# Setup of a one-layer transformer kernel: token rows spread by a matrix product, convolution weights quantised on GpSimd, embedding between parts of the Gram product

## The chip, the core and the metric

The kernel runs on one core of a Trainium2 chip. A core has five engines with an instruction stream each: TensorE (PE, matrix products, with its weight loads shown apart as PEld), VectorE (DVE), ScalarE (ACT), GpSimd (POOL) and SyncE (SP, which here only issues transfers). They share an on-chip memory of 128 partitions (SBUF) and an accumulator memory that TensorE writes (PSUM, 8 banks of 512 fp32 a partition), and meet at semaphores. The metric is the device time of one execution, in microseconds.

## The reference

Integer tokens of shape (2, 1024) go through an embedding with a short convolution, attention and a mixture of experts, each with a residual. Cut to what matters here:

```python
# embedding: both weights are quantised by their largest magnitude / 127
w_emb = fake_quant(emb_weight)                  # (125, 128)
e = w_emb[clip(y, 0)]
x = pad(e, one zero row in front)               # context of 2
w = fake_quant(conv_weight)                     # (128, 1, 2), one pair a channel
h = relu(e_before * w[0] + e * w[1])            # depthwise, per channel
# attention: 8 heads of 64, weights scaled by 1/sigma, one power iteration
v = W @ u / norm; u2 = W.T @ v / norm; sig = v @ W @ u2; Wq = W / sig * sigma
h = h + softmax(mask_diagonal(q k^T * exp(temperature))) v @ Wo.T + b_out
h = h + mixture_of_experts(layernorm(h))
```

`fake_quant(w)` is `w + (round(w / scale) * scale - w)` with `scale = max|w| / 127`.

## The kernel before

The kernel is written per engine, with the order on each engine and every semaphore wait by hand. No planner decides anything.

The layer's body is eight head pairs (four for each of the two sequences). A pair is two heads of eight steps; a step `(k, t)` makes the scores of query tile `t` against all 1024 keys (TensorE, as high and low parts), takes the row maximum (VectorE), exponentials (ScalarE), divides (GpSimd), transposes the probabilities three steps later (TensorE, copied by ScalarE and VectorE), and multiplies them with the values five to six steps later. The projections of the next pair stand between the steps. After the pairs come the experts. None of this is touched but the first step.

The setup in front of it is what the change is about. The stages, with the engine that runs them:

- SP issues the transfers in one queue: embedding table, convolution weights broadcast to 128 partitions, the 1024 tokens of sequence 0 broadcast to 128 partitions, the attention weights by rows (`wr_sb`), the tokens of sequence 1, then all other weights. ScalarE issues the power-iteration vectors `u` and three scalars.
- GpSimd makes constants (`const`, 15 of them: `ones`, `ident`, masks, `vocab_id`, `tie`, `powers`).
- VectorE finds the largest magnitude of each row of the embedding table, and of the convolution weights; `quantise` is four instructions in a chain. The largest over all rows comes from a product on TensorE (`top`). `rows_of(b)` compares each of the 1024 tokens with the partition's number `vocab_id`: a one-hot matrix, vocabulary by position. `table` holds embedding times convolution weight, two taps; both are done at semaphore value `SETUP_TABLES`.
- TensorE: `top`; the Gram product of the 12 row blocks of W, then times `u` (`gu_ps`), which gives W.T W u and so both norms without the transposed pass; `embed(c)` for `c` = 0..3, each eight products (two taps, four tiles of 128 positions) of one-hot columns with `table`; `v_ps`, the output weights times their `u`; the transposes of the normalised first sequence; the projections `dk0`, `dk1`, `dq0`, `dq1` of head 0 (key and query, half 0 and 1); `u2_ps`; and the first scores.
- ScalarE copies each PSUM result: `embedded(c)` with the rectifier, `xt`, the high parts.
- VectorE takes statistics and normalises (`tile_statistics`, `variances`, `normalise_tile`, in groups `NORMS`), GpSimd takes the roots (`deviations`), and VectorE forms the low parts (`first_low`).

`embed(2)` and `embed(3)` are the second sequence, which isn't needed for the first head pair: its statistics are taken in steps (0, 2) to (0, 6) of pair 0.

## Time and profile before

| | us |
|---|---|
| median of 3 runs | 495.35 (495.01 to 495.76) |
| the profiled execution | 495.01 |
| its span, first to last instruction | 493.2 |
| PE / PEld busy | 472.3 (96%) / 404.6 (82%) |
| DVE / ACT / POOL busy | 423.6 (86%) / 363.8 (74%) / 300.6 (61%) |

Over the span the granted TensorE clock is 1.000. The chain that ended last is to 81% TensorE, to 13% VectorE, 2% each waiting for issue, DMA and ScalarE. The busy shares are averages: in the first 12.3 us (a fortieth of the span) TensorE is busy for two tenths of the time, VectorE five, ScalarE one, GpSimd two, and from the second slice on TensorE is at nine tenths or more until near the end. Times in all rows are from the first instruction of the span. A timeline row is: start, length, engine, line, operation, output<-input, count, and in brackets the idle time before it and what ended it. Rows that overlap on TensorE are passes in its pipeline: an fp32 product is two MATMUL records.

### The profile page before, as it was taken

The numbers are of one execution on the slowest core, as the hardware profiler recorded it, in microseconds if no ns is written. First come the engines' busy times: TensorE is split into PE (matmuls) and PEld (weight loads), VectorE is DVE, ScalarE is ACT, GpSimd is POOL, SyncE is SP. The second block draws the span as 40 slices with busy tenths as digits, with TensorE's granted clock in tenths as the row PEclk, the third lists the DMA queues.
The fourth block names the chain that finished last, engine by engine and source line by source line (L and its number), as shares of the span: only waits on it lengthen the run. The fifth ranks groups of instructions, "written<-read, shape, count | busy, mean of one in ns | idle before, by whom it ended". The sixth has DMA issues, their size and how long they took to land.

```text
span 493.2 us, 11360 instructions
## 1 busy us (share of the span) xinstructions
PE 472.3 (96%) x3824; PEld 404.6 (82%) x3824; DVE 423.6 (86%) x722; ACT 363.8 (74%) x688; POOL 300.6 (61%) x357
## 2 busy tenths in 40 slices
PE   2989999999999999999999999999999999999897
PEld 2945788888988898888788898889888988888685
DVE  5469989988998898889998999899989999999465
ACT  1258878887788778877888688878887887683553
POOL 2114697888668866874468857885788556751000
DMA  6500009531953195362622592259225932000002
GB/s 233 218 1 0 2 15 213 127 87 36 200 116 85 34 200 120 85 131 52 126 66 68 108 202 59 73 105 204 56 72 105 202 69 64 0 2 3 3 17 73
DMA packets 29484, 44.78 MB, mean 91 GB/s; under 512 B 3200, under 2 KB 21120, under 8 KB 29184
## 3 DMA queue, kind: packets, MB, share of 16 engines
q1 hardware_dynamic: 28864, 44.21, 38.4%
q8 instruction: 25, 0.41, 0.4%
q14 instruction: 19, 0.16, 0.1%
q10 hardware_dynamic: 576, 0.00, 0.1%
HBM read 6.46 MB, written 1.05 MB: 15 GB/s over the span
## 4 chain that ended last, share of the span: by engine, by line
PE 81%; DVE 13%; issue 2%; DMA 2%; ACT 2%; SPq 0%; POOL 0%; DVEq 0%; ACTq 0%
PE ps L696 22%; PE ps L680 19%; PE ps L662 10%; PE ps L663 10%; PE ps L603 5%; DVE pt_lo L1361 4%; DVE neg_max L1377 4%; PE ps L739 3%; PE ps L598 2%; PE ps L887 2%; DMA arena<-in_wqkv_rows 2%; PE ps L870 2%; PE ps L573 1%; DVE x L1198 1%; PE ps L901 1%
## 5 line engine op out<-in xcount | busy, mean ns | idle before, releaser
L1361 DVE TENSOR_TENSOR pt_lo<-ps,pt_hi 128x512 fp32r<-128x512 f32 x256 | 163.5, 680 | 1.3 <-ACT pt_hi L1036 1.3
L1377 DVE TENSOR_REDUCE neg_max<-ps 128x1 f32<-128x1024 f32 x128 | 156.6, 1223 | 6.5 <-PE ps L667 2.6
L1036 ACT ACTIVATE pt_hi<-ps 128x512 fp32r<-128x512 f32 x256 | 139.3, 596 | 29.4 <-PE ps L680 29.2
L438 POOL TENSOR_SCALAR probs<-probs,inv_sum 128x1024 f32<-128x1024 f32 x128 | 144.6, 1129 | 26.6 <-POOL inv_sum L435 26.6
L696 PE MATMUL ps<-pt_hi,v_slot 128*128 128x256 f32 x512 | 150.0, 324 | 0.0
L1056 ACT ACTIVATE probs<-ps,neg_max 128x1024 f32<-128x1024 f32 x128 | 142.5, 1113 | 6.9 <-DVE neg_max L1377 4.0
L680 PE MATMUL ps<-ident,probs 128*128 128x128 f32 x1024 | 133.7, 273 | 1.5 <-DVE pt_lo L1361 0.9
L680 PEld LDWEIGHTS ps<-ident,probs 128*128 128x128 f32 x1024 | 117.6, 140 | 19.8 <-POOL probs L438 3.0
L696 PE MATMUL ps<-pt_lo,v_slot 128*128 128x256 f32 x512 | 127.8, 282 | 0.0
L435 POOL TENSOR_TENSOR inv_sum<-row_sum,powers 128x1 f32<-128x1 f32 x128 | 70.8, 553 | 83.2 <-ACT probs L1056 83.2
L696 PEld LDWEIGHTS ps<-pt_hi,v_slot 128*128 128x128 f32 x512 | 96.8, 189 | 9.7 <-issue 9.7
L696 PEld LDWEIGHTS ps<-pt_lo,v_slot 128*128 128x128 f32 x512 | 96.7, 189 | 8.8 <-issue 8.8
L662 PE MATMUL ps<-k_hi,q_st 128*128 128x512 f32 x256 | 102.7, 401 | 0.9 <-DVE q_st L1232 0.9
L663 PE MATMUL ps<-k_lo,q_st 128*128 128x512 f32 x256 | 100.8, 394 | 0.0
L1369 DVE TENSOR_TENSOR ps<-ps,neg_block 128x128 f32<-128x128 f32 x112 | 33.4, 298 | 27.3 <-PE ps L663 26.9
L662 PEld LDWEIGHTS ps<-k_hi,q_st 128*128 128x128 f32 x256 | 48.0, 187 | 7.4 <-DVE q_st L1232 1.0
L663 PEld LDWEIGHTS ps<-k_lo,q_st 128*128 128x128 f32 x256 | 48.1, 188 | 6.8 <-issue 1.0
L1049 ACT ACTIVATE arena<-ps 128x256 f32<-128x256 f32 x64 | 24.7, 386 | 36.0 <-PE ps L696 36.0
L428 POOL TENSOR_TENSOR arena<-arena 128x512 fp32r<-128x512 f32 x28 | 35.9, 1282 | 5.2 <-POOL arena L426 5.0
L603 PE MATMUL ps<-xt,w_slot 128*128 128x512 f32 x56 | 28.7, 595 | 0.0
L1056 ACT ACTIVATION_READ_ACCUMULATOR probs<-ps,neg_max 128x1 f32 x128 | 25.3, 198 | 0.0
L395 POOL TENSOR_TENSOR rstd<-rstd,powers 128x4 f32<-128x4 f32 (+1 forms) x6 | 7.5, 1243 | 26.7 <-DVE rstd L1195 26.7
(145 smaller groups left out, 391.6 us busy)
## 6 DMA issues: line engine op xcount, KB each, us to landing
q_st<-arena SPq DMA_DIRECT2D x28, 256.0 KB, 3.8
k_hi<-arena SPq DMA_DIRECT2D x28, 256.0 KB, 5.1
k_lo<-arena SPq DMA_DIRECT2D x28, 256.0 KB, 5.2
v_slot<-v_all SPq DMA_DIRECT2D x14, 512.0 KB, 3.9
arena<-arena SPq DMA_DIRECT2D x28, 256.0 KB, 4.9
f_sb<-in_f SPq DMA_DIRECT2D x2, 1024.0 KB, 10.1
x<-in_tok SPq DMA_DIRECT2D x2, 512.0 KB, 7.6
w_slot<-in_w_pairs SPq DMA_DIRECT2D x8, 128.0 KB, 2.0
```

Source lines behind the costliest of these rows:

```text
L428: pool.tensor_tensor(low.bitcast(F32R), low, high, ALU.subtract).then_inc(qk_split, 1)
L435: pool.tensor_tensor(inv_sum[:, t % 4:t % 4 + 1], row_sum[:, t % 4:t % 4 + 1], powers[:, 3 * NT:3 * NT + 1], ALU.pow).then_inc(recip_done, 1)
L438: pool.tensor_scalar(probs[:, t % 4, :], probs[:, t % 4, :], inv_sum[:, t % 4:t % 4 + 1], 1.0, ALU.mult, ALU.mult).then_inc(norm_done, 1)
L603: return pe.matmul(ps[:, WORK, :], w_slot[:, which, :], xt[:, c * HALF:(c + 1) * HALF], start=True, stop=True)
L662: pe.matmul(bank, q, k_hi[:, k, half], start=True, stop=False)
L663: ins = pe.matmul(bank, q, k_lo[:, k, half], start=False, stop=c != own or not by_pe)
L680: ins = pe.transpose(ps[:, bank, q * P:(q + 1) * P], probs[:, (t - T_LAG) % 4, col:col + P], ident[:, :])
L696: ins = pe.matmul(ps[:, PV_BANK, 0:CW], v_slot[:, slot, jt, :], src[:, c_local % 2, jt, :], start=jt == 0 and src is pt_hi, stop=jt == NT ...
L1036: act.activation(dst, ps[:, transposes_bank(t, a, drain), :].rearrange("p (j c) -> p j c", c=P), ACT.Copy).then_inc(hi_done, 1)
L1056: act.activation(probs[:, t % 4, :].rearrange("p (a c) -> p a c", a=2), ps[:, SCORES + 2 * (t % 2):SCORES + 2 * (t % 2) + 2, :], ACT.Exp, ...
L1361: dve.tensor_tensor(pt_lo[at], ps[:, transposes_bank(t, a, drain), :].rearrange("p (j c) -> p j c", c=P), pt_hi[at].bitcast(F32), ALU.subt ...
L1377: dve.tensor_reduce(neg_max[:, t % 4:t % 4 + 1], ps[:, SCORES + 2 * (t % 2):SCORES + 2 * (t % 2) + 2, :].rearrange("p a c -> p (a c)"), AX ...
```

## The change

1. **Tokens.** The two broadcasts of 512 KB are gone. One transfer puts the tokens as 16 rows of 128 (`tok_sb`, 8 KB). GpSimd clamps them to fp32 and, in `tokens_apart(b)`, writes for each sequence a 16x1024 matrix `tok_diag` that holds row k's tokens in column block k and zero elsewhere (in the memory of `q_st`). `spread_tokens(b)` on TensorE multiplies it by a matrix of ones, which puts all tokens of a sequence on every partition of two PSUM banks, and VectorE makes the one-hot rows from there, in two halves.
2. **Convolution weights.** Their transfer goes first on ScalarE's queue, the tokens second, in front of `u` and the scalars. The scale is still VectorE's; the four instructions of the quantisation are GpSimd's, between `tokens_apart(0)` and `tokens_apart(1)`.
3. **Constants.** GpSimd makes the five that are needed first, and the others after all this; the waits are split accordingly (`N_FIRST_CONST`).
4. **TensorE's order.** Four Gram products, `embed(0)`, tokens of sequence 1, `embed(1)`, the other eight Gram products, `embed(2)`, then `gu_ps`. `embed(3)` is moved behind the first scores. `v_ps` is moved from in front of the transposes to between the projections. The first head's projections are in the order dk0, dq0, dk1, dq1 and in other banks.
5. **ScalarE and VectorE** follow that order; on VectorE `rows_of(1)` is behind the first group's statistics; on ScalarE in the first step the exponentials come before the value copies.

On TensorE, from the first product to the first projection, before (`quant` with `ones` is `top`, `arena` is the Gram product, `table` with `probs` an embedding product, `wo_sb` is `v_ps`, `ident` the transposes):

```order
L568 MATMUL ps<-quant,ones 128x125 [waits setup_dve,const_ready]
L573 MATMUL ps<-arena 128x128 [waits rows_loaded]
L573 MATMUL ps<-arena 128x128 x11
L578 MATMUL ps<-u_sb,arena 128x1 [waits setup_act,u_loaded]
L561 MATMUL ps<-table,probs 128x128 [waits one_hot_ready,setup_dve]
L562 MATMUL ps<-table,probs 128x128
...
L588 MATMUL ps<-u_sb,wo_sb 128x1 [waits wout_loaded]
L588 MATMUL ps<-u_sb,wo_sb 128x1 x3
L593 MATMUL ps<-ident,arena 128x128 [waits xhat_done] x8
L609 MATMUL ps<-xt,arena 128x512 [waits xt_done,h_ready,twice_loaded]
```

and after (`q_st` with `ones_r` spreads tokens):

```order
L617 MATMUL ps<-quant,ones 128x125 [waits setup_dve,const_ready]
L599 MATMUL ps<-q_st,ones_r 128x512 [waits tok_ready]
L605 MATMUL ps<-arena 128x128 [waits rows_loaded]
L605 MATMUL ps<-arena 128x128 x3
L590 MATMUL ps<-table,probs 128x128 [waits one_hot_ready,setup_dve]
...
L599 MATMUL ps<-q_st,ones_r 128x512 [waits tok_ready]
...
L590 MATMUL ps<-table,probs 128x128 [waits one_hot_ready]
...
L605 MATMUL ps<-arena 128x128 x8
L590 MATMUL ps<-table,probs 128x128 [waits one_hot_ready]
...
L632 MATMUL ps<-u_sb,arena 128x1 [waits setup_act,u_loaded]
L612 MATMUL ps<-ident,arena 128x128 [waits xhat_done] x8
L648 MATMUL ps<-xt,arena 128x512 [waits xt_done,h_ready,twice_loaded]
```

The Gram product is cut in two, three of the four embedding groups stand in and behind it, the tokens of a sequence in front of each pair of groups, and `v_ps` is no longer in front of the transposes.

On GpSimd, all that stands between the start and the first root, after:

```order
L381 AFFINE_SELECT ident<-ident 128x128
L390 TENSOR_SCALAR tok_f<-tok_sb 16x128 [waits tok_loaded]
L395 TENSOR_TENSOR q_st<-tok_f,ident 16x1024 [waits tok_ready,const_ready]
L403 TENSOR_SCALAR quant<-conv_sb,qs 125x256 [waits setup_dve]
L405 TENSOR_SCALAR quant<-quant,qs 125x256 [waits conv_steps]
L407 TENSOR_TENSOR quant<-quant,conv_sb 125x256 [waits conv_steps]
L409 TENSOR_TENSOR quant<-conv_sb,quant 125x256 [waits conv_steps]
L395 TENSOR_TENSOR q_st<-tok_f,ident 16x1024
L412 MEMSET ident_b 128x128
...
L424 TENSOR_SCALAR tie<-tie 128x16
L431 TENSOR_TENSOR rstd<-rstd,powers 128x4 [waits aggr_done] x2
```

Before, only the constants stood there (the first root came right behind them). Now the clamp, two spreads of 16x1024 and the four steps on 125x256 do, and the second spread follows the last step with no wait of its own.

On TensorE, the first scores (`k_hi`, `k_lo` with `q_st`) and what follows them, after:

```order
L707 MATMUL ps<-k_hi,q_st 128x512 [waits h_ready,first_lo,const_ready]
L708 MATMUL ps<-k_lo,q_st 128x512
L712 MATMUL ps<-ident_b,neg_diag 128x128
L590 MATMUL ps<-table,probs 128x128
L591 MATMUL ps<-table,probs 128x128
...
L637 MATMUL ps<-wv_sb,xt 128x512 [waits wv_loaded]
L637 MATMUL ps<-wv_sb,xt 128x512 [waits h_ready]
L768 MATMUL ps<-norm_sb,ones 128x2 [waits setup_dve]
```

Before, the rows of `table` weren't there, and the value products (`wv_sb`) followed at once.

The diff, cut to its core:

```diff
+        top, gram_ps, gu_ps = ps[:, 2, 0:VOCAB], ps[:, 3, 0:P], ps[:, 3, 0:1]
+        sums_ps, v_ps, u2_ps, out_sums_ps = ps[:, WORK, 0:2], ps[:, WORK, 4:5], ps[:, WORK, 8:12], ps[:, WORK, 0:2]
...
+        tok_diag = q_st[0:TILES, :, :].rearrange("k b (t n) -> k b t n", n=P)
...
-        EMBED_BANKS = (0, 1, 2, WORK)
-        FIRST_HEAD = {"dk0": WORK, "dk1": TRANS, "dq0": 2, "dq1": TRANS + 1}
+        TOKEN_BANKS = TRANS
+        EMBED_BANKS = (0, 1, 2, TRANS)
+        FIRST_HEAD = {"dk0": 0, "dq0": 1, "dk1": 3, "dq1": TRANS + 1}
...
+            const(pool.memset(ident[:, :], 0.0))
+            pool.wait_ge(const_ready, count[0])
+            const(pool.affine_select(out=ident[:, :], in_=ident[:, :], compare_op=ALU.not_equal, fill=1.0,
+                                     base=0, pattern=[[-1, P]], channel_multiplier=1))
             const(pool.memset(ones[:, :], 1.0))
-            const(pool.memset(ident[:, :], 0.0))
+            const(pool.memset(ones_r[:, :].bitcast(F32), 1.0))
+            const(pool.iota(vocab_id[:, :], [[0, 1]], base=0, channel_multiplier=1,
+                            allow_small_or_imprecise_dtypes=True))
+            assert count[0] == N_FIRST_CONST
+
+            pool.wait_ge(tok_loaded, 16)
+            pool.tensor_scalar(tok_f[:, :], tok_sb[:, :], float(VOCAB - 1), 1.0, ALU.min, ALU.mult).then_inc(tok_ready, 1)
+            pool.wait_ge(const_ready, 2)
+            pool.wait_ge(tok_ready, 1)
+            def tokens_apart(b):
+
+                pool.tensor_tensor(tok_diag[:, b, :, :], tok_f[:, :].unsqueeze(1).broadcast_to([TILES, NT, P]),
+                                   ident[0:TILES, NT * b:NT * (b + 1)].unsqueeze(2).broadcast_to([TILES, NT, P]),
+                                   ALU.mult).then_inc(tok_ready, 1)
+
+            tokens_apart(0)
+            conv_flat = conv_sb[0:VOCAB, :, :].rearrange("p k d -> p (k d)")
+            conv_q = quant[0:VOCAB, D:3 * D]
+            pool.wait_ge(setup_dve, SETUP_CONV)
+            pool.tensor_scalar(conv_q, conv_flat, qs[0:VOCAB, 6:7], ROUND, ALU.mult, ALU.add).then_inc(conv_steps, 1)
+            pool.wait_ge(conv_steps, 1)
+            pool.tensor_scalar(conv_q, conv_q, ROUND, qs[0:VOCAB, 4:5], ALU.subtract, ALU.mult).then_inc(conv_steps, 1)
+            pool.wait_ge(conv_steps, 2)
+            pool.tensor_tensor(conv_q, conv_q, conv_flat, ALU.subtract).then_inc(conv_steps, 1)
+            pool.wait_ge(conv_steps, 3)
+            pool.tensor_tensor(conv_q, conv_flat, conv_q, ALU.add).then_inc(conv_steps, 1)
+
+            tokens_apart(1)
...
-            for m, fill in ((ident, 1.0), (ident_b, 1.0), (neg_diag, NEG), (neg_block, NEG)):
+            for m, fill in ((ident_b, 1.0), (neg_diag, NEG), (neg_block, NEG)):
...
-            sp.dma_start(conv_sb[:, :, :].rearrange("p k d -> p (k d)"),
-                         conv.rearrange("(o k) d -> o (k d)", o=1).partition_broadcast(P)).then_inc(conv_loaded, 16)
-            def tokens(b):
-                sp.dma_start(tok_sb[b], tok[b:b + 1, :].partition_broadcast(P)).then_inc(tok_loaded[b], 16)
-
...
-            tokens(0)
             sp.dma_start(wr_sb, wqkv_rows).then_inc(rows_loaded, 16)
-            tokens(1)
...
+            def spread_tokens(b):
+
+                pe.wait_ge(tok_ready, b + 2)
+                for c in range(2):
+                    pe.matmul(ps[:, TOKEN_BANKS + 2 * b + c, :], ones_r[:, :],
+                              tok_diag[:, b, 4 * c:4 * c + 4, :], start=True, stop=True).then_inc(tok_mm, 1)
...
+            pe.wait_ge(const_ready, N_FIRST_CONST)
             pe.wait_ge(setup_dve, SETUP_DIAG)
             pe.matmul(top, ones[0:VOCAB, :], quant[0:VOCAB, 0:VOCAB], start=True, stop=True).then_inc(setup_pe, 1)
-
-
+            spread_tokens(0)
             pe.wait_ge(rows_loaded, 16)
-            for t in range(12):
-                last = pe.matmul(gram_ps, wr_sb[:, t, :], wr_sb[:, t, :], start=t == 0, stop=t == 11)
-            last.then_inc(setup_pe, 1)
-
+            gram(0, 4)
+            pe.wait_ge(setup_dve, SETUP_TABLES)
+            pe.wait_ge(one_hot_ready, 2)
+            embed(0).then_inc(h_mm, 1)
+            spread_tokens(1)
+            pe.wait_ge(one_hot_ready, 3)
+            embed(1).then_inc(h_mm, 1)
+            gram(4, 12).then_inc(setup_pe, 1)
+            pe.wait_ge(one_hot_ready, 5)
+            embed(2).then_inc(h_mm, 1)
             pe.wait_ge(u_loaded, 16)
             pe.wait_ge(setup_act, 2)
             pe.matmul(gu_ps, gram_sb, u_sb[:, 0:1], start=True, stop=True).then_inc(setup_pe, 1)
-
-            pe.wait_ge(setup_dve, SETUP_TABLES)
-            for c in range(4):
-                if c % 2 == 0:
-                    pe.wait_ge(one_hot_ready, c + 2)
-                embed(c).then_inc(h_mm, 1)
-
-            pe.wait_ge(wout_loaded, 32)
-            for j in range(H // 2):
-                last = pe.matmul(v_ps, wo_sb[:, j, :], u_sb[:, 1 + j:2 + j], start=j == 0, stop=j == H // 2 - 1)
-            last.then_inc(setup_pe, 1)
-
-            for t in range(NT):
-                pe.wait_ge(xhat_done, t + 1)
-                ins = pe.transpose(ps[:, 5 + t // 4, (t % 4) * P:(t % 4 + 1) * P], x_hat[0][:, t, :], ident[:, :])
-                if t % 4 == 3:
-                    ins.then_inc(xt_mm, 1)
+            transpose_rows(0)
+            transpose_rows(1)
...
             pe.wait_ge(twice_loaded, 16)
-            pe.wait_ge(h_ready, 4)
+            pe.wait_ge(h_ready, 2)
             for kind, bank in FIRST_HEAD.items():
-                pe.wait_ge(xt_done, int(kind[2]) + 1)
-                if kind == "dk1":
-                    pe.wait_ge(setup_act, 4)
+                pe.wait_ge(xt_done, 2 if kind == "dq1" else int(kind[2]) + 1)
                 project_twice(kind, 0, bank).then_inc(first_mm, 1)
                 if kind == "dk0":
-
+                    pe.wait_ge(one_hot_ready, 6)
                     pe.wait_ge(setup_dve, SETUP_PRODUCTS)
                     pe.matmul(sums_ps, ones[:, :], norm_sb[:, 18:20], start=True, stop=True).then_inc(setup_pe, 1)
-
-            pe.wait_ge(xt_done, 2)
+                if kind == "dq0":
+                    pe.wait_ge(wout_loaded, 32)
+                    pe.wait_ge(setup_dve, SETUP_RATIO)
+                    for j in range(H // 2):
+                        last = pe.matmul(v_ps, wo_sb[:, j, :], u_sb[:, 1 + j:2 + j], start=j == 0, stop=j == H // 2 - 1)
+                    last.then_inc(setup_pe, 1)
+
+            pe.wait_ge(setup_act, 4)
             for t in range(4):
                 last = pe.matmul(u2_ps[:, t:t + 1], wor_sb[:, t * P:(t + 1) * P], norm_sb[:, 12:13],
                                  start=True, stop=True)
             last.then_inc(setup_pe, 1)
+            pe.wait_ge(const_ready, N_CONST)
 
             def first_values(t):
 
                 for i in (2 * t, 2 * t + 1):
                     if i == 0:
-                        pe.wait_ge(setup_act, 5)
-                    if i == 0:
                         pe.wait_ge(wv_loaded, 16)
+                    if i == 1:
+                        pe.wait_ge(h_ready, 4)
                     if i == 2:
                         pe.wait_ge(first_lo, 4)
...
+                if pair.i == 0 and (k, t) == (0, 0):
+                    embed(3).then_inc(h_mm, 1)
...
+            act.dma_start(conv_sb[:, :, :].rearrange("p k d -> p (k d)"),
+                          conv.rearrange("(o k) d -> o (k d)", o=1).partition_broadcast(P)).then_inc(conv_loaded, 16)
+            act.dma_start(tok_sb[:, :], tok.rearrange("b (t n) -> (b t) n", n=P)).then_inc(tok_loaded, 16)
...
+            embedded(0)
+            embedded(1)
             act.wait_ge(setup_pe, 2)
             act.activation(gram_sb, gram_ps, ACT.Copy).then_inc(setup_act, 1)
+            embedded(2)
             act.wait_ge(setup_pe, 3)
             act.activation(norm_sb[:, 0:1], gu_ps, ACT.Copy).then_inc(setup_act, 1)
-            for c in range(4):
-                embedded(c)
-            act.wait_ge(setup_pe, 4)
-            act.activation(norm_sb[:, 12:13], v_ps, ACT.Copy).then_inc(setup_act, 1)
-            for c in range(2):
-                act.wait_ge(xt_mm, c + 1)
-                act.activation(xt[:, c * HALF:(c + 1) * HALF], ps[:, 5 + c, :], ACT.Copy).then_inc(xt_done, 1)
+            rows_copied(0)
+            rows_copied(1)
...
+                if kind == "dq0":
+                    act.wait_ge(setup_pe, 5)
+                    act.activation(norm_sb[:, 12:13], v_ps, ACT.Copy).then_inc(setup_act, 1)
...
+                            if t == 0:
+                                embedded(3)
+                                exponentials(pair, k, t)
                             first_values(t)
-                            exponentials(pair, k, t)
+                            if t > 0:
+                                exponentials(pair, k, t)
...
-            dve.wait_ge(const_ready, N_CONST)
+            dve.wait_ge(const_ready, 2)
...
-            quantise(conv_flat, quant[0:VOCAB, D:3 * D], 1)
-
-            def rows_of(b):
-
-                dve.wait_ge(tok_loaded[b], 16)
-                dve.wait_ge(const_ready, N_CONST)
-                dve.memset(one_hot[b][:, 0:1], 0.0).then_inc(one_hot_ready, 1)
-                dve.tensor_scalar(one_hot[b][:, 1:SEQ + 1], tok_sb[b], float(VOCAB - 1), vocab_id[:, :],
-                                  ALU.min, ALU.is_equal).then_inc(one_hot_ready, 1)
-
-            rows_of(0)
+            assert count[0] == SETUP_CONV
             dve.wait_ge(setup_pe, 1)
             link(dve.tensor_reduce(qs[0:VOCAB, 1:2], top[0:VOCAB, :], AXX, ALU.max))
             scale(0)
             quantise(emb_sb[0:VOCAB, :], quant[0:VOCAB, 0:D], 0)
+
+            def rows_of(b):
+
+                dve.wait_ge(const_ready, N_FIRST_CONST)
+                dve.memset(one_hot[b][:, 0:1], 0.0).then_inc(one_hot_ready, 1)
+                for c in range(2):
+                    dve.wait_ge(tok_mm, 2 * b + c + 1)
+                    dve.tensor_scalar(one_hot[b][:, 1 + HALF * c:1 + HALF * (c + 1)], ps[:, TOKEN_BANKS + 2 * b + c, :],
+                                      vocab_id[:, :], None, ALU.is_equal).then_inc(one_hot_ready, 1)
+
+            rows_of(0)
...
+                if g == 0:
+                    rows_of(1)
...
-            first_low("dk0")
-            dve.wait_ge(setup_pe, 5)
+            dve.wait_ge(setup_pe, 4)
             ratio(0, sums_ps)
             assert count[0] == SETUP_RATIO
-            first_low("dk1")
+            first_low("dk0")
             dve.wait_ge(setup_pool, 1)
...
-            first_low("dq0")
-            first_low("dq1")
+            for kind in ("dq0", "dk1", "dq1"):
+                first_low(kind)
```

## Rows read from the trace of the kernel before

**Rows 1.** The chain that ended last, to 50 us: start, length, what.
```profile
2.14 7.91 DMA arena<-in_wqkv_rows
...
10.10 4.84 PE ps L573 x24
...
16.06 0.22 PE ps L562 x2
...
22.98 0.79 PE ps L588 x8
...
30.67 0.50 PE ps L662
...
39.52 0.37 ACT v_slot L997
```

**Rows 2.** L573 (ns min/median/max) at 12 and 14 us; busy time with PEclk.
```profile
L573 PE MATMUL ps<-arena x6: 421/421/421, 11.8 to 12.8; 128*128 128x128 f32 x6
...
L573 PE MATMUL ps<-arena x8: 274/275/421, 13.7 to 14.6; 128*128 128x128 f32 x8
...
12.00:13.00 1.00, 1.00 (x6) 1.00 (x6) 0.28 (x1) 0.00 (x0) 0.00 (x0) 1.00 1.06 376
```

**Rows 3.** Transfers by us from issue to landing; one issue.
```profile
arena<-in_wqkv_rows SPq DMA_DIRECT2D x1, 768.0 KB, 7.9
...
conv_sb<-in_conv SPq DMA_DIRECT2D x1, 128.0 KB, 3.6
...
u_sb<-in_u_cols ACTq DMA_DIRECT2D x1, 2.5 KB, 2.1
...
sig<-in_sigma_qkv ACTq DMA_DIRECT2D x1, 0.5 KB, 3.8
...
sig<-in_temperature ACTq DMA_DIRECT2D x1, 0.5 KB, 8.1
...
1.20 0.46 ACTq L942 DMA_DIRECT2D sig<-in_sigma_qkv  x1
```

**Rows 4.** Groups on GpSimd, whole run: busy, mean ns of one.
```profile
L438 POOL TENSOR_SCALAR probs<-probs,inv_sum 128x1024 f32<-128x1024 f32 x128 | 144.6, 1129 | 26.6 <-POOL inv_sum L435 26.6
...
L428 POOL TENSOR_TENSOR arena<-arena 128x512 fp32r<-128x512 f32 x28 | 35.9, 1282 | 5.2 <-POOL arena L426 5.0 <-ACT probs L1056 0.2
...
L411 POOL TENSOR_TENSOR h_sb<-h_sb,b_sb 128x1024 f32<-128x1024 f32 x2 | 4.8, 2400 | 0.0
...
L388 POOL TENSOR_SCALAR tie<-tie 128x16 f32<-128x16 f32 x1 | 0.2, 211 | 0.0
```

**Rows 5.** L1198 at 74 and 70 us, and what GpSimd did.
```profile
L1198 DVE TENSOR_SCALAR x<-h_sb,mv,rstd x2: 333/755/1177, 75.1 to 76.2; 128x128 f32<-128x128 f32 x2
...
L1198 DVE TENSOR_SCALAR x<-h_sb,mv,rstd x2: 333/626/918, 71.7 to 72.5; 128x128 f32<-128x128 f32 x2
...
71.21 1.29 POOL L428 TENSOR_TENSOR arena<-arena 128x512 fp32r<-128x512 f32 x1 [0.19 <-POOL arena L426]
...
75.06 1.13 POOL L438 TENSOR_SCALAR probs<-probs,inv_sum 128x1024 f32<-128x1024 f32 x1 [0.21 <-POOL inv_sum L435]
```

**Rows 6.** VectorE: two groups of the whole run, and two timeline rows.
```profile
L1460 DVE TENSOR_SCALAR probs<-ps 128x512 f32<-128x512 f32 x1 | 0.7, 691 | 1.5 <-PE ps L852 1.5
...
L1156 DVE TENSOR_TENSOR quant<-quant,emb_sb 125x128 f32<-125x128 f32 x1 | 0.3, 293 | 0.0
...
18.29 0.87 DVE L1185 BATCH_NORM_STATS2 stats<-h_sb 128x6 f32<-128x128 f32 x4 [6.01 <-ACT h_sb L946]
...
19.08 0.36 DVE L1192 BATCH_NORM_AGGREGATE mv<-stats 128x2 f32<-128x6 f32 x4
```

**Rows 7.** TensorE's timeline at the first head: start, length.
```profile
25.05 1.10 PE L609 MATMUL ps<-xt,arena 128*128 128x512 f32 x2 [0.34 <-ACT xt L961]
...
26.12 2.82 PE L609 MATMUL ps<-xt,arena 128*128 128x512 f32 x6
...
28.78 0.95 PE L625 MATMUL ps<-norm_sb,arena 128*128 128x1 f32 x8
```

36 lines of the change are left out of this document (25 added, 11 removed).

## The prediction

> **What bounds the kernel now.** The change touches only the first 42 us or so of the 493, so I first read the chain that ended last over its start [rows 1]. SP issues transfers, the chain stands on the landing of the attention weights until 10.05, and from 10.10 on it is almost all TensorE: the Gram product (4.84 us), four embedding groups (0.22 a product), the product with the output weights (0.79), transposes, the first head's projections, and the first scores at 30.67. It stays on TensorE until about 39.5, then goes over to ScalarE and VectorE. So before 10 us an engine other than TensorE has slack, and between 10 and 39 us whatever is put on or taken off TensorE counts in full.
>
> The second view is TensorE's own rows [rows 2]. The granted clock reads 1.00 throughout, but a pass of the Gram product lasts 421 ns at 12 us and 275 at 14: the pace of 1.2 GHz for the first 3.8 us of work after an idle stretch, that of 2.4 GHz from about 13.9. A 128-column fp32 product (two passes) costs 0.40 us slow (4.84 for 12) and 0.22 fast [rows 1].
>
> Third, the transfers [rows 3]. The k-th transfer of ScalarE's queue lands about with the k-th of SP's: its first (u, issued 0.75) at 2.85, its second (sigma_qkv, issued 1.20) at 5.0 beside the second of SP, conv (issued 1.21) at 4.8, its fourth (temperature, issued 2.16) at 10.3 beside SP's fourth, the rows, at 10.05.
>
> **What the change does to the start, step by step** (times from the start of the span).
>
> *Transfers.* The token broadcasts (512 KB each) and conv leave the way of the rows, so these land before 10.05, and even 10.05 would do (below). The 16x128 tokens go second on ScalarE's queue, issued about 1.2. Their landing T isn't in the trace: the first transfer of that queue landed at 2.85, the second at 5.0 [rows 3]; only eight packets per DMA engine stand ahead of them, so I take T = 4.0. The temperature is needed once an embedding is done; it is now the sixth transfer of its queue, but SP's first six hold 1.5 MB, as much as its first four before (1.4 MB, landed at 10.05), so it comes before 13.
>
> *GpSimd before the table.* Its first constants (ident, ones, vocab_id) are done by 2. Then: clamp 16x128, 0.2 us (L388's 0.21); the diagonal spread of 16x1024, a TENSOR_TENSOR, 2.4 (L411; it walks the 1024 columns, and 16 partitions instead of 128 save nothing in my estimate; bounds 1.1 by L438 and 2.6 by twice L428); 0.2 between dependent instructions [rows 4]. Start 4.05, end 6.85. Then the four steps on 125x256: 0.35 for each TENSOR_SCALAR, 0.65 for each TENSOR_TENSOR, scaled by columns from the same rows: 2.0, plus three gaps of 0.2, plus what follows.
>
> *VectorE against GpSimd.* VectorE's L1198, SBUF to SBUF, lasts 333 ns by itself but 1177 ns when issued at 75.1 under GpSimd's L438 (75.06 to 76.19): it ended just after GpSimd. The same at 71.7: 918 ns, to just after L428 ended at 72.50 [rows 5]. So quantising the embedding table (two TENSOR_SCALAR, two TENSOR_TENSOR of 0.29 [rows 6]), which is ready at about 5.8, waits for the spread (6.85) and then takes turns with GpSimd's conv steps. I charge 0.5 for the turns: conv done at 9.95. One-hot rows from PSUM, 2 x 0.62 (0.69 for such an instruction, less overlap [rows 6]), are done about 10.7.
>
> *The tables.* They need conv done, two TENSOR_TENSOR with both inputs in SBUF. But behind the last conv step GpSimd has, with no wait between, the second spread of 2.4 us. Whether it blocks a TENSOR_TENSOR no row shows: the bounds are 0 (tables done 10.7 + 0.65 = 11.35) and the whole of it (9.95 + 2.4 + 0.65 = 13.0). I take 13.0, since the nearest rows are a VectorE instruction that reads and writes SBUF under GpSimd's elementwise ones. The Trainium skill ("SBUF — State Buffer", section "Who interferes with whom") says that a DVE instruction with two SBUF inputs contends with a GpSimd instruction that reads SBUF, and that the second to issue fully blocks; no run here shows it for two inputs, and by it the sum is the one with 13.0. Before, the tables were done at 11.49 and hidden under the Gram product.
>
> *TensorE after that.* Token product (0.9 slow) and four of twelve Gram products (4 x 0.40) run from 6.9 to 9.4, hidden. Then it idles 3.6 us, so I take the slow pace again for the next 3.8: embedding 0 is 8 x 0.40 = 3.2 (13.05 to 16.25), token product 0.85 (17.1), embedding 1 8 x 0.22 = 1.78 (18.9), eight Gram products 1.76 (20.65), embedding 2 (22.45), gu 0.35 (22.8). VectorE must have x_hat by then: embedded 0 copied 16.85, statistics 0.87 and 0.36 [rows 6] and the rest 0.2 (18.3), the moved one-hot rows 1.25 (19.55), second statistics 1.45 (21.0), four normalised by 22.2: in time. Transposes 4 x 0.13 (23.3), copy 0.6, first projection at 24.05, against 25.05 before [rows 7]: 1.0 earlier.
>
> *To the first scores.* Before, 5.6 (25.05 to 30.67). Now four projections at 0.86 (three last 2.82 to the end of the third [rows 7]), the product with the output weights 0.8 (moved here), u2 0.85 and the sums 0.12 fill TensorE without a gap: 5.2. Scores at 29.25, 1.4 earlier. The scalar chain (ratio, root, scales, 1.6 us) runs beside the projections.
>
> *Given back.* Embedding 3, 1.78, now stands between the first scores and the first values, on TensorE where the chain still is [rows 1]. Value tile 1 waits for ScalarE's copy of it (0.6, under value tile 0); on ScalarE the copy and the first exponentials (1.1 + 0.2) precede the value copies, so the output ratio, for which the second head's first projection waits, comes some 0.4 later. Given back: 2.2.
>
> *Sum.* -1.4 + 2.2 = +0.8. The profiled execution took 495.01 (span 493.2), the median is 495.35; with +0.8 on the median the forecast is 496.1. From the first values on nothing is changed, and the steady part takes the shift as it comes.
>
> **Rivals.**
> 1. *The second spread doesn't block the tables.* The turns cost less too: tables at 10.45. TensorE has been idle only 1 us and may keep its clock; with half of the slow penalty embedding 0 ends at 12.95, token product (GpSimd's second spread ends by 12.1) 13.45, embedding 1 15.2, Gram 17.0, embedding 2 18.8. Now VectorE is last: copy 13.55, statistics 15.0, one-hot 16.3, statistics 17.75, four normalised 19.0; first projection 20.35, scores 25.55. -5.1 + 2.2 = -2.9; with the whole slow penalty -2.1. About 492.8 (492.2 to 493.6). For it: no instruction of two SBUF inputs is seen blocked; against: the rows of blocked neighbours.
> 2. *Slower: the tokens land late.* Everything in the chain above hangs on T one for one, since GpSimd does one thing after another up to the tables. If T is that of the second transfer in this queue, 5.0 [rows 3], tables are done at 14.0, and +0.8 becomes +1.8; if the rows' packets hold them up to 6, +2.8. About 497.5. It decides from T above 4.2. For it: the queue's second transfer came 2.15 after its first, the two after it took 5.3 together [rows 3]; against: those went to 128 partitions each, the tokens to 16.
> A third outcome is inside the forecast's spread: the tables are blocked, but TensorE keeps the fast pace over its 3.6 us of idling. Then 1.42 and 0.4 come off, -1.0, 494.3. Against it stands that it began slow at 10.1 after an idle stretch (5.5 us, though).
>
> **How the numbers follow.** Forecast (blocked tables, T near 4) 0.48, its own range 494.3 to 497.2; rival 1 0.40; rival 2 0.12. Within 0.2% is 494.36 to 496.34, about what a measurement of this kernel tells from no change. The forecast gives 0.02 faster, 0.29 same, 0.17 slower; rival 1 0.37 faster, 0.03 same; rival 2 0.11 slower, 0.01 same. Together 0.39, 0.33, 0.28. The cases have both signs, so the range spans both: from 492.4, near the low end of rival 1, to 497.2.
>
> **What would show it.** In the changed profile: T where GpSimd's clamp starts (4.0); its spread 2.4 us long; VectorE's table products (L1240) waiting for conv and then one of them about 2.3 us long instead of 0.29, ending with GpSimd's second spread, which is the forecast against rival 1; embedding 0 starting at 13.05 (10.5 in rival 1) and its passes at 421 or 275 ns; first scores at 29.25; the second scores 2.2 later behind the first than before. The forecast is wrong if embedding 0 starts before 12, if the clamp starts after 5, or if the gap from first scores to the chain's point at 39.5 doesn't grow by about 2.

## The result

| | before | after |
|---|---|---|
| median | 495.59 (494.86 to 501.28, 20 runs) | 501.14 (498.72 to 505.47, 20 runs) |
| ratio | | 1.0092, 95% interval 1.0068 to 1.0116 |
| the profiled execution, its span | 495.01, 493.2 | 505.47, 503.7 |
| first scores | 30.67 | 35.24 |
| fourth row maximum of the first head | 43.85 | 50.42 |

The change makes the kernel 0.9% slower: 5.5 us on the medians, against a forecast of +0.8 and a range that ended at 497.2. The executions of the changed kernel lie in groups: eight at 498.7 to 499.6, nine at 500.8 to 501.4, three at 502.8 to 505.5. The last group, the profiled one among it, has a dip of the granted clock near the end that executions of the kernel before have too, so its span is read here without that: 6.6 us are there by the fourth row maximum, and the other 3.9 of the span's 10.5 come at 470 to 485 us.

The rows of the first 45 us stand first. The chain that ended last, after the change (start, length, what), answers to [rows 1]:

```profile
0.75 5.20 DMA conv_sb<-in_conv
...
7.92 1.81 DVE quant L1214
9.73 0.59 POOL quant L403
10.42 1.17 POOL quant L405
11.66 0.74 POOL quant L407
12.46 0.73 POOL quant L409
13.22 1.97 DVE table L1240
15.22 0.30 DVE table L1240
...
24.20 2.11 PE ps L605 x16
...
29.50 1.10 PE ps L648 x2
...
35.24 0.47 PE ps L707
```

Before, the chain stood on the landing of the attention weights until 10.05 and mostly on TensorE from there. Now TensorE isn't on it before 15.56: it runs over the convolution weights' transfer, VectorE, GpSimd's four steps and VectorE's tables. The two spreads aren't on it themselves, but L1214 and the first L1240 are as long as they are because of them, as the next rows show. So nearly all that the change put on GpSimd sets the time of the tables.

GpSimd's and VectorE's timelines (start, length, engine, line, operation, then the idle time before and its releaser):

```profile
6.89 0.66 POOL L390 TENSOR_SCALAR tok_f<-tok_sb 16x128 f32<-16x128 int32 x1 [5.00 <-DMA tok_sb<-in_tok]
...
7.70 1.93 POOL L395 TENSOR_TENSOR q_st<-tok_f,ident 16x1024 fp32r<-16x1024 f32 x1 [0.15 <-POOL tok_f L390]
7.92 1.80 DVE L1214 TENSOR_SCALAR quant<-quant,qs 125x128 f32<-125x128 f32 x1
...
13.14 1.89 POOL L395 TENSOR_TENSOR q_st<-tok_f,ident 16x1024 fp32r<-16x1024 f32 x1
13.22 2.29 DVE L1240 TENSOR_TENSOR table<-quant 125x128 f32<-125x128 f32 x2 [1.30 <-POOL quant L409]
```

The tokens are there at 6.8, not at 4.0. The first table product is issued 0.08 us after the second spread, and lasts 1.97 instead of 0.30, until that spread is over: the forecast's mechanism, against rival 1. For the table product, which has two inputs in SBUF, this is what the Trainium skill ("SBUF — State Buffer", section "Who interferes with whom") says of such an operation of VectorE under GpSimd's. VectorE's L1214 has one tensor as input and is held under the first spread all the same (1.80 instead of 0.29).

The transfers (KB each, us from issue to landing) answer to [rows 3]:

```profile
conv_sb<-in_conv ACTq DMA_DIRECT2D x1, 128.0 KB, 5.2
...
tok_sb<-in_tok ACTq DMA_DIRECT2D x1, 8.0 KB, 5.6
```

conv, issued at 0.75, took 5.2 (before, behind the embedding table, 3.6), and 8 KB issued behind it at 1.19 took 5.6.

TensorE's embedding passes (count, ns min/median/max, first and last start), in embedding 0, embedding 1 and embedding 2, answer to [rows 2]:

```profile
L590 PE MATMUL ps<-table,probs x8: 421/421/582, 15.6 to 18.5; 128*128 128x128 f32 x8
...
L590 PE MATMUL ps<-table,probs x8: 421/421/582, 20.4 to 23.4; 128*128 128x128 f32 x8
...
L590 PE MATMUL ps<-table,probs x8: 275/275/275, 26.2 to 27.6; 128*128 128x128 f32 x8
```

and the stretch between them (PE, PEld, DVE, ACT, POOL busy, PEclk, DMA share, GB/s):

```profile
20.00:24.00 4.00, 4.00 (x19) 3.58 (x17) 2.65 (x12) 0.00 (x0) 1.05 (x1) 1.00 0.00 0
```

TensorE runs at the pace of 1.2 GHz from 15.56 to 24.7: two embeddings, a token product and the first passes of the Gram product that follows at 24.0. It had not been faster before. These are its products from 9 us to the first of embedding 0, and the passes of the first four Gram products (421 ns, so slow already in front of the idle stretch that ends at 15.56):

```profile
9.68 1.21 PE L599 MATMUL ps<-q_st,ones_r 16*128 16x512 f32 x2 [3.77 <-POOL q_st L395]
10.83 2.08 PE L605 MATMUL ps<-arena 128*128 128x128 f32 x8
15.56 0.80 PE L590 MATMUL ps<-table,probs 128*128 128x128 f32 x2 [2.66 <-DVE table L1240]
```

```profile
L605 PE MATMUL ps<-arena x8: 421/421/582, 10.8 to 12.5; 128*128 128x128 f32 x8
```

So the idle stretch did not bring the pace down; it was never up. In every trace here TensorE is slow from its first product on and rises once in the first 25 us, after which the setup stays fast. The PEclk column reads 1.00 all the while, since the trace has no clock record before 24.77. The first record, at 24.77, is a rise to 1.00, just where the passes change. Before the first record the passes tell the pace, not the column. The Trainium skill ("TensorE: Matmul & The Clock Gate", section "Seeing it yourself") warns that recorded clock events have been seen to be unreliable; here the recorded rise fits the passes, and it is the level before it that is missing.

The row maxima, by which the shift is read, fourth of the first head, before and after:

```profile
43.85 1.21 DVE L1377 TENSOR_REDUCE neg_max<-ps 128x1 f32<-128x1024 f32 x1
```

```profile
50.42 1.21 DVE L1438 TENSOR_REDUCE neg_max<-ps 128x1 f32<-128x1024 f32 x1
```

From here on both kernels run in step (next maximum 4.28 later in both). The dip near the end, in the expert stage, in the same columns as above, after and then before:

```profile
470.00:475.00 5.00, 3.65 (x48) 3.05 (x50) 1.98 (x3) 1.57 (x3) 0.00 (x0) 0.69 0.02 3
475.00:480.00 5.00, 5.00 (x104) 5.00 (x100) 1.38 (x3) 1.17 (x3) 0.00 (x0) 0.50 0.01 3
480.00:485.00 5.00, 4.74 (x169) 4.31 (x169) 3.11 (x5) 3.17 (x6) 0.00 (x0) 0.78 0.00 0
```

```profile
475.00:480.00 5.00, 5.00 (x115) 4.34 (x112) 3.39 (x7) 2.28 (x4) 0.00 (x0) 1.00 0.11 30
```

Here the column does show it: 0.50 is the level of 1.2 GHz. The clock records of this trace put it at 0.50 from 471.9 to 482.2.

### The profile page after: what moved, and what is told of

The parts are those of the page before. It is cut to its first block, busy times and chain, and to the rows that moved or that the text cites. A ratio compares the mean times of both kernels' runs of the same rounds, so it can differ in the third digit from the quotient of the medians.

```text
span 503.7 us, 11376 instructions
## 1 busy us (share of the span) xinstructions
PE 482.1 (96%) x3828; PEld 412.5 (82%) x3828; DVE 427.1 (85%) x720; ACT 363.7 (72%) x688; POOL 308.5 (61%) x365
## 4 chain that ended last, share of the span: by engine, by line
PE 80%; DVE 14%; ACT 2%; issue 2%; DMA 1%; POOL 1%; DVEq 0%
PE ps L741 21%; PE ps L725 19%; PE ps L708 10%; PE ps L707 10%; PE ps L642 5%; DVE neg_max L1438 4%; DVE pt_lo L1422 4%; PE ps L786 3%; PE ps L917 2%; PE ps L934 1%; PE ps L637 1%; PE ps L590 1%; PE ps L591 1%; DMA conv_sb<-in_conv 1%; PE ps L887 1%
## 5 line engine op out<-in xcount | busy, mean ns | idle before, releaser
L725 PEld LDWEIGHTS ps<-ident,probs 128*128 128x128 f32 x1024 | 117.7, 140 | 19.5 <-POOL probs L474 2.6
L1104 ACT ACTIVATE arena<-ps 128x256 f32<-128x256 f32 x64 | 24.7, 386 | 35.9 <-PE ps L741 35.9
```

Of the source, the lines that this page charges most:

```text
L725: ins = pe.transpose(ps[:, bank, q * P:(q + 1) * P], probs[:, (t - T_LAG) % 4, col:col + P], ident[:, :])
```

## The experiments

Of each profiled execution: the first scores, the fourth row maximum, both as start times, the latter against 43.85, and the span against 493.2. "Dip" marks a trace in which PEclk falls near the end.

| kernel | first scores | fourth maximum | span | median against before |
|---|---|---|---|---|
| after | 35.24 | 50.42 (+6.57) | 503.7 (+10.5), dip | 1.0092 |
| 1 tokens first | 31.24 | 46.41 (+2.56) | 499.5 (+6.3), dip | 1.0083 |
| 2 second spread late | 33.03 | 48.19 (+4.34) | 501.3 (+8.1), dip | 1.0071 |
| 3 conv on VectorE | 34.37 | 49.54 (+5.69) | 498.7 (+5.5) | 1.0075 |
| 4 after, kept busy | 30.88 | 46.05 (+2.20) | 501.2 (+8.0), dip | 1.0122 |
| 5 before, kept busy | 28.98 | 42.15 (-1.70) | 492.6 (-0.6) | 0.9999 |
| 6 embedding 3 in the setup | 34.32 | 48.50 (+4.65) | 497.9 (+4.7) | 1.0131 |
| 7 before, embedding 3 late | 30.10 | 45.30 (+1.45) | 494.7 (+1.5) | 1.0029 |
| 8 transfers mended | 30.64 | 45.81 (+1.96) | 495.3 (+2.1) | 1.0037 |
| 9 the same, kept busy | 27.33 | 42.50 (-1.35) | 492.3 (-0.9) | 1.0017 |
| 10 the same, conv on VectorE | 28.18 | 43.35 (-0.50) | 493.4 (+0.2) | 1.0009 |
| 11 as 9, embedding 3 in the setup | 29.33 | 43.49 (-0.36) | 497.3 (+4.1), dip | 1.0044 |
| 12 as 9, values first | 27.13 | 42.17 (-1.68) | 496.2 (+3.0), dip | 0.9984 |

Two things are read from the table as a whole. A delay at the fourth maximum reaches the end one for one (3, 6, 7 and 8 within 0.2), a gain only in part (5: 0.6 of 1.70; 9: 0.9 of 1.35) or not at all (10: a gain of 0.50 ends as a loss of 0.2). What eats the gains isn't shown. And the dip is worth 3.7 to 5.8 us by itself (the span's shift less the fourth maximum's), whatever the kernel. Ratios differ by which share of the executions has it (3 of the 29 of before that ran beside kernels 3, 10 and 11; 4 of 6 of kernel 4), so the traces tell the mechanisms apart better than the medians do.

**1. The order of two transfers.**

```diff
+            act.dma_start(tok_sb[:, :], tok.rearrange("b (t n) -> (b t) n", n=P)).then_inc(tok_loaded, 16)
             act.dma_start(conv_sb[:, :, :].rearrange("p k d -> p (k d)"),
                           conv.rearrange("(o k) d -> o (k d)", o=1).partition_broadcast(P)).then_inc(conv_loaded, 16)
-            act.dma_start(tok_sb[:, :], tok.rearrange("b (t n) -> (b t) n", n=P)).then_inc(tok_loaded, 16)
```

> The changed kernel with the token transfer first and conv second on ScalarE's queue (the one edit). In the changed kernel the tokens landed at 6.8 us, conv at 5.95, and the spread of the tokens on GpSimd starts 0.8 after the tokens. Theory (the chain to the tables starts with the tokens, one for one): tokens land about 3 to 4, conv at about 6.2, first spread at 4.5, conv steps from 7.3 (after VectorE's scale, which waits for conv), tables at about 13.3 instead of 15.5, the whole 2 us less than the changed kernel, about 498. Rival (conv and VectorE's scale are as late as the tokens, so the other input of the conv steps takes over): tables only some 0.5 to 1 earlier, 500 to 500.6. Rival (the loss is not in the start): no change.

Measured: 499.79 (10 runs), ratio 1.0083 (1.0054 to 1.0112). GpSimd's and VectorE's timelines of this kernel:

```profile
2.88 0.66 POOL L390 TENSOR_SCALAR tok_f<-tok_sb 16x128 f32<-16x128 int32 x1 [0.99 <-DMA tok_sb<-in_tok]
```

```profile
7.51 0.42 DVE L1220 TENSOR_REDUCE qs<-conv_sb 125x1 f32<-125x256 f32 x1 [3.84 <-DMA conv_sb<-in_conv]
```

The tokens come 4.0 us earlier, so their lateness was nothing but the place behind conv. But conv then comes 1.4 later and is the next wait, and the second spread holds the tables as before (1.96): embedding 0 starts at 14.29, a gain of 1.27: between the theory's 2.2 and the rival. The executions without the dip say the same, group against group (497.5 to 498.0 against 499.2, 499.6 to 500.6 against 501.2: 1.3 to 1.5 less). The first scores of the trace move by 4.0, more than that, because the pace rises at 17.57 here, right behind embedding 0 (below), which isn't the edit's doing.

**2. The second spread behind the tables.**

```diff
+            pool.wait_ge(setup_dve, SETUP_TABLES)
             tokens_apart(1)
```

> The changed kernel, in which GpSimd waits for the tables before it spreads the tokens of sequence 1 (the one edit). Theory (a VectorE instruction with two SBUF inputs is held for the whole of GpSimd's spread): the first table product takes 0.29 instead of 1.97 us, embedding 0 starts 1.7 earlier at 13.8, the second spread runs 13.8 to 15.7 under embedding 0, the whole is 1.7 less, about 499.4. Rival (the 1.97 us have another cause, such as a late start behind the semaphore): the table product stays at about 2 us and nothing changes.

Measured: 499.68 (12 runs), ratio 1.0071 (1.0033 to 1.0108). The two table products of this kernel (ns min/median/max):

```profile
L1241 DVE TENSOR_TENSOR table<-quant x2: 291/292/293, 12.7 to 13.0; 125x128 f32<-125x128 f32 x2
```

0.62 us for both instead of 2.29, and embedding 0 at 13.38 instead of 15.56. Of these 2.2 us the edit gives 1.7; the other 0.5 is there because the tokens landed 0.5 earlier in this execution (clamp at 6.42). The spread itself is hidden under embedding 0 (13.41 to 15.3). This settles the disputed step: GpSimd's TENSOR_TENSOR of 16x1024 holds VectorE's of 125x128 with two SBUF inputs until it is over.

**3. The conv steps back on VectorE** (second part of the change undone; tokens stay behind conv).

```diff
-            pool.wait_ge(setup_dve, SETUP_CONV)
-            pool.tensor_scalar(conv_q, conv_flat, qs[0:VOCAB, 6:7], ROUND, ALU.mult, ALU.add).then_inc(conv_steps, 1)
...
-            assert count[0] == SETUP_CONV
+            quantise(conv_flat, quant[0:VOCAB, D:3 * D], 1)
```

> The changed kernel with part 2 half undone: the four steps of the convolution weights' quantisation are VectorE's again (behind their scale, ahead of the embedding's maximum), their transfer stays first on ScalarE's queue. Theory A (GpSimd's serial chain of clamp, spread and 3.45 us of conv steps is what delays the tables): without the steps GpSimd's two spreads end at about 9.6 and 11.6, the tables are done near 12.5 instead of 15.5, embedding 0 starts near 12.6, about 498.5. Theory B (VectorE is as late, since its own steps with two SBUF operands are held by the two spreads, 7.7 to 11.6, and it then has eight quantising steps and two one-hot halves in a row): conv steps end at 11.6 to 11.9, the embedding's at 13.3, one-hot 14.8, tables 15.4, so embedding 0 starts within 0.5 us of 15.56 and the time stays near 501. I hold B.

Measured: 500.3 (12 runs), ratio 1.0075 (1.0039 to 1.0111). The last conv step, now VectorE's:

```profile
L1205 DVE TENSOR_TENSOR quant<-conv_sb,quant x1: 2001/2001/2001, 8.3 to 8.3; 125x256 f32<-125x256 f32 x1
```

It is held under the first spread (2.0 instead of 0.42), and the embedding's first step under the second (1.09 instead of 0.28). The tables are done at 15.17, 0.34 earlier than in the changed kernel, so theory B stands. The tokens landed 0.3 later in this execution (clamp at 7.21 instead of 6.89), so the offload costs some 0.7 us in front of the tables: no help while the tokens are late, and a small part of the loss.

**4 and 5. TensorE kept busy**, 8 and 14 products of 128 columns without use in the changed kernel (before the tokens' product and before the tables' wait), 14 in the kernel before ahead of the Gram product.

```diff
+            def keep_busy(n):
+                for _ in range(n):
+                    pe.matmul(ps[:, 0, 0:P], ones[:, :], ones[:, :], start=True, stop=True)
```

> The changed kernel with products of ones into an unused bank on TensorE where it idles: 8 behind the product that finds the largest magnitude (5.9 us), 14 behind the first four Gram products. They compute nothing that is used. Theory (TensorE falls to its slow pace because it idles in front of embedding 0, and then runs embeddings 0 and 1 and the token product at 0.43 a product instead of 0.22): these run at the fast pace, embedding 0 in 1.8 instead of 3.8, embedding 1 in 1.8 instead of 3.8, token product 0.5 instead of 1.15: 4.6 less, 496.5, if VectorE does not then hold the transposes, with which 3 to 4 less. Rival (the pace rises by the time since the start of the program or in a way that idle time does not govern): the pace rises at the same time, about 24 us, and the products added cost up to 2 us: 501 to 503.

> The kernel before, with 14 products of ones into an unused bank on TensorE between the product that finds the largest magnitude (4.6 us) and the Gram product (10.1). They compute nothing that is used. Theory (idle time in front of a stretch of products costs the slow pace for its first 4 us or more; the Gram product paid it before): the Gram product takes 2.7 instead of 4.84 us, first scores at 28.6, the whole 2.1 less, 492.9. Rival (the pace is regained by the same time whatever TensorE did before): no change, or up to 0.5 more.

Measured: kernel 4 503.46 (6 runs), ratio 1.0122 (1.0075 to 1.0168); kernel 5 494.56 (12 runs), ratio 0.9999 (0.9973 to 1.0026). Embedding 0's passes in kernel 4, and the Gram product in kernel 5:

```profile
L590 PE MATMUL ps<-table,probs x8: 275/275/377, 15.5 to 17.0; 128*128 128x128 f32 x8
```

```profile
10.28 2.94 PE L578 MATMUL ps<-arena 128*128 128x128 f32 x24 [0.91 <-DMA arena<-in_wqkv_rows]
```

In kernel 4's stretches at 465 and 470 us (PE, PEld, DVE, ACT, POOL busy, PEclk, DMA share, GB/s):

```profile
465.00:470.00 5.00, 4.14 (x79) 3.93 (x80) 1.20 (x2) 1.80 (x4) 0.00 (x0) 0.74 0.01 3
470.00:475.00 5.00, 4.22 (x72) 3.82 (x70) 2.06 (x4) 1.51 (x3) 0.00 (x0) 0.50 0.02 3
```

With the tables as late as ever (embedding 0 at 15.47), the first scores come 4.4 us earlier in kernel 4; from embedding 0 to them it takes 15.4 us instead of 19.7. The pace rose at 10.0, 4.9 us after TensorE's first product. In kernel 5 the Gram product takes 2.94 instead of 4.84 and the first scores come 1.7 earlier. So up to the first scores the slow pace cost 4.3 us in the changed kernel and 1.9 in the one before. The whole of kernel 4 doesn't show it: its profiled execution has the longest dip of all (0.50 from 467.4 to 481.0), and its two executions without a dip, at 498.3 and 499.3, lie 1 to 2 us above what its fourth maximum lets one expect (495.0 + 2.2 = 497.2). So it isn't shown that the 4.3 reach the end in full. Twelve executions of kernel 5 are 10 at 493.9 to 496.0 and 2 near 499.6; before has a median of 495.58.

**6 and 7. Embedding 3.** Kernel 6 puts it back into the setup behind embedding 2, kernel 7 moves it alone in the kernel before (with ScalarE's exponentials ahead of the value copies, as in the change).

```diff
             embed(2).then_inc(h_mm, 1)
+            pe.wait_ge(one_hot_ready, 6)
+            embed(3).then_inc(h_mm, 1)
...
-                if pair.i == 0 and (k, t) == (0, 0):
-                    embed(3).then_inc(h_mm, 1)
```

> The changed kernel with embedding group 3 back in the setup, behind group 2, and its ScalarE copy there too. Theory (moving it behind the first scores only shifts 1.8 us of TensorE work from one place of the chain to another, and costs some 0.2 to 0.4 more there through the order on ScalarE): first scores 1.8 later at 37.0, everything from the second step on 0 to 0.4 earlier, so 500.7 to 501.2. Rival (it is partly hidden in the first step): 0.5 to 1.5 more, up to 502.5.

> The kernel before, with only embedding group 3 moved behind the first scores, its ScalarE copy and the first exponentials in front of the value copies as in the changed kernel, and its bank changed to the one the changed kernel uses. Theory (a move within the chain): first scores 1.8 earlier at 28.9, scores of the second step at the same time or up to 0.4 later than before; the whole 495.3 to 495.8. Rival (part of the group hides in the first step): 494.3 or less.

Measured: kernel 6 502.36 (6 runs), ratio 1.0131 (1.0096 to 1.0166); kernel 7 496.51 (12 runs), ratio 1.0029 (1.0012 to 1.0047). TensorE's scores of the first and second step in kernel 7:

```profile
30.10 0.50 PE L664 MATMUL ps<-k_hi,q_st 128*128 128x512 f32 x1 [0.95 <-DVE q_st L1240]
...
35.00 0.47 PE L664 MATMUL ps<-k_hi,q_st 128*128 128x512 f32 x1
```

From first scores to the fourth maximum before has 13.2 us, all kernels with embedding 3 behind the scores 15.0 to 15.2, kernels 6 and 11 with it in the setup (and ScalarE's new order) 14.2. So eight products of 1.8 us in all, taken out of the setup, come back as 2.0: 1.0 of it goes with embedding 3, the other 1.0 with something else that was changed in the first step, ScalarE's order among it. No run has that order alone. In kernel 7 the first scores gain only 0.6, as the weight rows landed 0.4 later than before and the transposes wait for VectorE; by itself the move costs 1 us. Kernel 6 has the same start as the changed kernel, embedding 0 at 15.55, but its embedding 1 is fast:

```profile
L590 PE MATMUL ps<-table,probs x8: 275/275/377, 19.8 to 21.3; 128*128 128x128 f32 x8
```

From the start of embedding 0 to the rise it takes 3.3 us here (to 18.9) and in kernel 1 (14.3 to 17.6), but 8.1 to 9.2 in the changed kernel and in kernels 2, 3 and 8, at starts that differ in nothing I could find. From embedding 0 to the first scores the short case takes 17.0 us (kernel 1), the long one 19.1 to 19.7: 2.2 to 2.7 apart. That is about the distance of the two groups of executions, 499.2 and 501.2 in the changed kernel, 497.8 and 499.7 in kernel 1, 494.8 and 497.1 in kernel 8. Where a profiled execution without a dip can be placed, it fits: kernel 6 with the short case is in its lower group, kernels 3 and 8 with the long one are in their upper. For the changed kernel itself no execution of the lower group has a trace. The Trainium skill ("TensorE: Matmul & The Clock Gate", section "What's actually happening") states that the number of slow products varies from run to run; these groups agree.

**8 to 12. All mended, then its parts.** Kernel 8: tokens first on ScalarE's queue, conv second on SyncE's, second spread behind the tables. Kernel 9 adds 4, 2, 3 and 6 products without use. Kernel 10 is 9 with the conv steps on VectorE, 11 is 9 with embedding 3 in the setup, 12 is 9 with ScalarE's value copies ahead of the exponentials in the first step.

Kernel 8's new place of conv, on SyncE behind the embedding table, and kernel 12's edit on ScalarE:

```diff
+            sp.dma_start(conv_sb[:, :, :].rearrange("p k d -> p (k d)"),
+                         conv.rearrange("(o k) d -> o (k d)", o=1).partition_broadcast(P)).then_inc(conv_loaded, 16)
...
                                 embedded(3)
-                                exponentials(pair, k, t)
                             first_values(t)
-                            if t > 0:
-                                exponentials(pair, k, t)
+                            exponentials(pair, k, t)
```

> The changed kernel with the tokens first on ScalarE's queue, conv second on SP's queue as before the change, and the second token spread behind the tables. Theory (three costs in front of embedding 0: tokens late, conv late, tables held by the spread): tokens at 2.9, conv at about 5 instead of 5.95, GpSimd's conv steps 5.9 to 9.2, tables at 9.9 instead of 15.5; TensorE idles little in front of embedding 0, so the slow pace ends during it; first scores at about 27 instead of 35.2, and the whole 6 to 7 less than the changed kernel: 493 to 494.5, below the kernel before. Rival (the rows of the attention weights or the scalars, now behind, arrive later and hold TensorE or ScalarE): rows after 8 or the temperature after 12, and the whole 495 to 497.

> As the kernel with changed transfers and late second spread, and with products of ones on TensorE where it would idle (4, 2, 3 and 6 of them, before the largest magnitude's product, before and after the first token product, and behind the first Gram products); they compute nothing that is used. Theory: embedding 0 starts at 9.9 at the fast pace, first scores at 25 to 25.5, the whole 491 to 492, 3.5 to 4 below the kernel before. Rival (VectorE's chain of statistics, one-hot rows and normalisation holds the transposes once TensorE is fast): first scores at 26.5 or later, the same as without the added products within 0.5.

> The version with tokens first, conv second on SyncE's queue, second spread late and dummy products, and the conv steps on VectorE. Here no spread is at work when VectorE quantises. Theory B of the first kernel (VectorE's own list is long): conv steps 7.3 to 8.8, embedding's maximum, scale and steps to 10.7, one-hot halves 12.2, tables 12.8, embedding 0 near 12.9 instead of 11.9, so 1 us slower than with GpSimd, about 497. Theory A: GpSimd's steps were the limit (3.45 us), VectorE's take 1.5, tables near 10, embedding 0 near 10.4, about 494.5.

> Tokens first on ScalarE's queue, conv second on SyncE's, second spread behind the tables, dummy products of 4, 2, 3 and 6 to keep TensorE busy, and embedding 3 in the setup behind embedding 2 instead of behind the first scores. Theory: the move of embedding 3 is neutral, it costs 1.8 us of TensorE before the first scores (27.3 to 29.1) and gives back 2.0 behind them (second-step scores 32.20 to 32.1), so the time stays within 1 us of the version with embedding 3 behind the scores (495 to 496). Rival: behind the scores it costs more than its own products, since it delays the first values and ScalarE's copies, and then this version is 1 us or more faster, near 494.

> The version with tokens first, conv second on SyncE's queue, second spread late and dummy products, with one edit: in the first step ScalarE makes the value copies before the exponentials, as in the kernel before (embedding 3 stays behind the first scores). In all traces with the exponentials first, the fourth row maximum comes 14.2 us (embedding 3 in the setup) or 15.2 us (behind the scores) behind the first scores, against 13.2 in the kernel before. Theory A: of the 2.0 us given back, 1.0 is ScalarE's order and 1.0 embedding 3; then this version has 14.2 us, its fourth row maximum comes near 41.5 instead of 42.50, and the time is some 0.5 to 1 us below that version's (494.4 in the trace). Theory B: with embedding 3 ahead of them the values are late for ScalarE anyway, and the exponentials behind them only push the first head's probabilities back: the interval stays at 15.2 and the time the same.

Measured: kernel 8 497.16, ratio 1.0037 (1.0012 to 1.0061); kernel 9 496.16, 1.0017 (0.9987 to 1.0047); kernel 10 495.38, 1.0009 (0.9978 to 1.0040); kernel 11 498.6, 1.0044 (1.0014 to 1.0075); kernel 12 494.6, 0.9984 (0.9941 to 1.0026); 12 runs each. The table products of kernel 10 against the start of its embedding 0:

```profile
12.42 0.61 DVE L1237 TENSOR_TENSOR table<-quant 125x128 f32<-125x128 f32 x2
...
13.08 0.49 PE L582 MATMUL ps<-table,probs 128*128 128x128 f32 x2 [1.26 <-DVE table L1237]
```

Kernel 8 has embedding 0 at 11.45, 4.1 us earlier than the changed kernel but 1.5 later than expected, mostly as conv landed at 6.2 and not at 5. Its first scores are where they were before the change (30.64 against 30.67), since it still runs slow until 19.5. Kernel 9 is at the fast pace from 11.0 on and has them 3.3 us earlier than before, though at 27.3 and not at 25 to 25.5; two of the 3.3 are given back by the fourth maximum. In kernels 9 to 12 TensorE has products from 1.93 on, with no pause over 0.4 us, and the pace rises only at 10.2 to 11.5. Kernel 10's tables are 1.5 later than kernel 9's and its embedding 0 is 1.0 later (12.03 in kernel 9, where it also waits 0.4 behind the products without use): VectorE's own list is the longer one once nothing holds it, so there GpSimd's steps help. The whole times of the two don't differ by more than their intervals. In kernel 11 embedding 3 in the setup is 2.0 later at the first scores and 1.0 at the fourth maximum. Kernel 12 contradicts my theory A: the interval from first scores to fourth maximum is 15.04, not 14.2. So with embedding 3 behind the scores ScalarE's order is worth 0.1; whether it is the 1.0 that kernels 6 and 11 still lack without embedding 3 is open. No version beats the kernel before by more than its interval. The nearest are kernels 5 and 12.

## Why the prediction was wrong

The direction of the forecast's sum was right and its size was not: +0.8 forecast, 5.5 measured. The chances did not follow the sum: a slower kernel had 0.28, the least of the three. Two terms of the sum failed above all, the tokens' landing (+2.9) and the length of the slow pace (+2.6 up to the end of embedding 1). Step by step, forecast against trace, up to the first scores (29.25 forecast, 35.24 measured, 6.0 apart):

- **The tokens' landing T, 4.0 against 6.9: +2.9.** This is the step that failed worst, with the slow pace below. I reasoned that "only eight packets per DMA engine stand ahead of them" and set T below the 5.0 that [rows 3] show for the queue's second transfer. Kernel 1 shows that what stood ahead was the whole delay: first in the queue they are there at 2.9. It also shows that the term isn't additive: with the tokens in time, conv's landing is the next wait, and embedding 0 gains only 1.27. Rival 2 was this mechanism, but with conv's transfer at its old duration it stopped at T = 6, and had 0.12.
- **Clamp and spread, 2.8 against 2.74: 0.** Two errors cancel: the clamp takes 0.66 and not 0.2 (the row it was taken from has 16 columns and fp32, the clamp 128 and int32; which of the two costs isn't shown), the spread 1.93 and not 2.4.
- **The conv steps, 3.1 against 3.45: +0.35.**
- **Second spread and tables, 3.05 against 2.33: -0.7.** The mechanism was right (kernel 2 takes it away, and 1.7 us with it), the spread is shorter. Rival 1 is refuted.
- **Embedding 0 to the end of embedding 1, 5.85 against 8.44: +2.6.** The forecast had the slow pace for 3.8 us, because [rows 2] show 3.8 after one idle stretch. It lasted 9.2, so embedding 1 was slow as well (3.58 instead of 1.78). The other 0.8 is the price of slow products: 0.40 is an average over the twelve of the Gram product, of which the last were fast ([rows 2] show the rise at 13.9), while a product in the slow stretch takes 0.43; the token product took 1.15. The picture behind it failed too, that TensorE falls back to the slow pace by idling: it had never left it. That also answers the third outcome, in which it keeps the fast pace. Kernel 4 has no slow pass from embedding 0 on and 4.3 us less. What sets the length is open; if the lower group of executions is the one with the short case, the forecast's length was about right for it.
- **From there to the first projection, 5.15 against 5.5, and from it to the scores, 5.2 against 5.74: +0.9.** TensorE's one gap is the 0.34 in front of the first projection, where ScalarE copies. 0.4 of the 0.9 is the eight Gram products, whose first passes were still slow (2.16 instead of 1.76). 0.45 is the four projections: forecast 4 x 0.86 = 3.44, measured 3.89, and [rows 7] had shown 3.89 for the same four (25.05 to 28.94).
- **Given back, 2.2 against 2.0: -0.2.** Right, and kernel 7 shows it by itself. The second scores, named as a sign, are 1.9 later behind the first than before.

One reading of the rows was wrong as well, without a price here. The chain of the kernel before isn't on TensorE from 10.10 to 39.5: between the first projection and the first scores it runs over ScalarE and VectorE, so not all that is put on or taken off TensorE there counts in full.

```profile
27.26 0.61 ACT k_hi L970
...
29.07 0.70 ACT q_st L969
29.86 0.77 DVE q_st L1232
```

The sum is 2.9 + 0.35 - 0.7 + 2.6 + 0.9, about 6.0, and +0.8 + 6.0 - 0.2 = 6.6 is the fourth maximum's shift. The medians are 5.5 apart: the profiled execution of before is 0.6 below its median, and 0.5 stays unexplained. A clamp after 5 was named as what would make the forecast wrong, and it started at 6.89.

What would have come nearer from the same rows: the queue's second transfer at 5.0 was the nearest row and the change made its forerunner 50 times larger, so T should have been bounded by conv's landing (no earlier than 0.75 + 3.6 = 4.35, and later with the rows beside it), and rival 2 should have been the forecast. Even so it ends at +2.8. The long slow pace stands in no row of the kernel before, so the measured time could not have been had from them.

## What to carry to other kernels

A small transfer that a chain of engines waits for goes first in its queue, in front of any broadcast to 128 partitions. Elementwise work moved to GpSimd "because it is idle" has two prices, its own slowness on the chain (3.5 us for four steps that VectorE does in 1.7) and VectorE's operations held until it is over; give it a wait if what is behind it can wait. A kernel's first products can all run at the slow pace, whatever the clock column says before its first record: read the passes, and price the products of a setup as slow until a row shows the rise. Filling TensorE's idle time brought the rise forward and took 4.3 us off the way to the first scores here, but the whole kernel did not gain clearly by it. And what is moved behind the setup comes back if TensorE is the bound there too.

## What the runs showed that I had not expected

- TensorE starts slow in every trace and rises once, between 7.9 and 24.8 us. From the start of the work that it rises in, it took 3.3 to 4.9 us in kernels 1, 4, 5, 6, 7 and before, and 8.1 to 9.6 in the changed kernel and kernels 2, 3, 8 and 9 to 12, nothing between. In kernels 9 to 12 that is work with no pause over 0.4 us, counted from 1.93, so idling alone doesn't make the long case. In kernel 10 an idle stretch of 1.26 us behind the rise was followed by fast passes.
- Near the end PEclk falls to 0.50 in some executions of every kernel, for 10.2 us in five of the six traces that have it and 13.7 in kernel 4's; it costs 3.7 to 5.8 us. It was in 3 of 29 executions of before, 3 of 20 of the changed kernel, but in 4 of 6 of kernel 4 and 6 of 12 of kernel 11. Whether products without use make it more frequent isn't settled: kernel 5, with 14 of them, has 2 of 12.
- A transfer of 8 KB in 16 rows takes 2.0 us when first in its queue (kernel 1) and 5.6 behind a broadcast of 128 KB. The broadcast itself took 3.6 before and 4.8 to 6.2 in all kernels with the change's transfers; why isn't shown.
- GpSimd's 16x128 clamp of int32 takes 0.66 us, three times its 128x16 operation on fp32 [rows 4], which has an eighth of the columns; the 16x1024 spread 1.9, less than a 128x1024 operation of the same kind (2.4) but by far not an eighth.
